# Second layer's experts: the odd batches' additions move from VectorE to GpSimd

## The reference, cut to what matters

```python
def _L1_ffn_ref(hidden_states, gate_w, w1, b1, w2, b2):
    x = hidden_states.reshape(-1, h)
    gate_probs = jax.nn.softmax(x @ gate_w.T, axis=-1)
    expert_idx = jnp.argmax(gate_probs, axis=-1)
    expert_w = jnp.take_along_axis(gate_probs, expert_idx[:, None], axis=1)[:, 0]
    for e in range(n_experts):
        ye = jax.nn.relu(x @ w1[e] + b1[e]) @ w2[e] + b2[e]
        sel = (expert_idx == e)[:, None]
        out = out + jnp.where(sel, ye * expert_w[:, None], 0.0)
...
x = x + jnp.tanh(g_ffn[1]) * _L1_ffn_ref(_layernorm(x, axis=-1), L1_ffn_gate_w, ...)
x = x + jnp.tanh(g_xattn[2]) * _L2_xattn_ref(_layernorm(x, axis=-1), ctx_1024, ...)
```

## Time and profile before

| | us |
|---|---|
| median of 3 runs | 1598.94 |
| lowest and highest of them | 1594.63, 1601.74 |
| the profiled execution | 1602.53 |
| its span (first to last instruction) | 1600.8 |
| PE, DVE, ACT, POOL busy | 1386.6, 953.2, 664.8, 422.6 |

### The profile page before, as it was taken

How to read it: one execution, slowest core, us unless ns; L and a number is a source line. 1 busy time by engine, 2 the same in 40 slices (tenths; PEclk the granted TensorE clock), 3 DMA queues, 4 the chain that set the end, 5 groups by cost and what they waited for, 6 DMA issues and landing times. The chain is left out here.

```text
span 1600.8 us, 31601 instructions
## 1 busy us (share of the span) xinstructions
PE 1386.6 (87%) x10662; PEld 1150.0 (72%) x10662; DVE 953.2 (60%) x2331; ACT 664.8 (42%) x1313; POOL 422.6 (26%) x578
## 2 busy tenths in 40 slices
PE   8999878889999994999999998999999997401588
PEld 5888645677799983788888887779999996400245
DVE  4888665666422225777777774832222265688887
ACT  3666453420344430333333334335555522430277
POOL 1000000012122210122221221246666633421141
PEclk9999999899799997999999998889999999755799
DMA  3000020673111107111111202012333344421001
GB/s 107 21 20 15 6 92 1 218 268 61 60 34 41 34 22 226 62 51 49 49 47 32 44 1 93 1 52 92 92 93 93 86 173 134 108 19 10 1 14 40
DMA packets 105328, 106.53 MB, mean 67 GB/s; under 512 B 36080, under 2 KB 92160, under 8 KB 105088
## 3 DMA queue, kind: packets, MB, share of 16 engines
q1 hardware_dynamic: 89312, 70.91, 14.6%
q0 software_dynamic: 11136, 28.93, 6.6%
q10 hardware_dynamic: 4768, 5.25, 1.1%
HBM read 83.19 MB, written 20.71 MB: 65 GB/s over the span
## 5 line engine op out<-in xcount | busy, mean ns | idle before, releaser
L3598 PEld LDWEIGHTS L2f_bank<-L2f_xT,L2f_w_tile 128*128 128x128 f32 x1264 | 154.5, 193 | 7.4 <-ACT L2f_xT L3662 3.4
L3598 PE MATMUL L2f_bank<-L2f_xT,L2f_w_tile 128*128 128x128 f32 x1264 | 155.2, 276 | 3.0 <-ACT L2f_xT L3662 3.0
L785 POOL TENSOR_TENSOR L2x_probs<-L2x_probs,L2x_inv_sum 128x512 f32<-128x512 f32 x64 | 66.3, 1057 | 268.4 <-DVE L2x_inv_sum L1062 268.4
L3712 DVE TENSOR_TENSOR L2f_hT<-L2f_gate_h,L2f_bank 128x256 f32<-128x256 f32 x79 | 33.3, 421 | 148.5 <-ACT L2f_gate_h L3669 148.5
L3521 POOL DMA_INDIRECT L2f_y_rows<-L2f_xn,L2f_put_row x79 | 78.2, 989 | 55.2 <-DVE L2f_xn L3728 51.6
L3656 ACT COPY L2f_w_tile<-L2f_w_up 128x1024 f32 x79 | 82.7, 1046 | 17.4 <-issue 17.4
L3513 POOL DMA_INDIRECT L2f_rows<-L2f_x_rows,L2f_take_row x79 | 77.0, 975 | 44.7 <-DVE L2f_take_row L3496 21.3
L3598 PEld LDWEIGHTS L1f_bank<-L1f_xT,L1f_w_tile 128*128 128x128 f32 x736 | 85.6, 192 | 1.1
L3598 PE MATMUL L1f_bank<-L1f_xT,L1f_w_tile 128*128 128x128 f32 x736 | 85.9, 275 | 0.0
L3615 PE MATMUL L1f_bank<-L1f_w_down,L1f_hT 128*128 x368 | 83.1, 379 | 0.0
L3615 PE MATMUL L2f_bank<-L2f_w_down,L2f_hT 128*128 x316 | 81.4, 380 | 0.1
(11 more groups left out here) (677 smaller groups left out, 3321.2 us busy)
## 6 DMA issues: line engine op xcount, KB each, us to landing
L1f_w_up<-in_L_ffn_w SPq DMA_DIRECT2D x16, 512.0 KB, 8.2
L1f_w_down<-in_L_ffn_w SPq DMA_DIRECT2D x16, 512.0 KB, 9.0
L2f_got<-L2f_y_rows SPq DMA_DIRECT2D x16, 512.0 KB, 4.4
L2f_w_up<-in_L_ffn_gate_w SPq DMA_DIRECT2D x16, 256.0 KB, 2.9
L2f_w_up<-in_L_ffn_up_w SPq DMA_DIRECT2D x16, 256.0 KB, 3.0
L2f_w_down<-in_L_ffn_down_w SPq DMA_DIRECT2D x16, 256.0 KB, 3.6
x<-in_x SPq DMA_DIRECT2D x4, 512.0 KB, 7.9
L0x_ctx<-in_ctx SPq DMA_DIRECT2D x16, 128.0 KB, 2.1
```

Of the source, the lines that this page charges most:

```text
L785: nc.gpsimd.tensor_tensor(probs[c][:, :, :], probs[c][:, :, :], inv_sum[:, c, :][:, :, None].to_broadcast([P, 4, P]), ALU.mult).then_inc(s ...
L3598: x = nc.tensor.matmul(products(j, m), w_tile[j][:, at:at + P], xT[j][:, k * P:(k + 1) * P], start=(k == 0), stop=(k == KT - 1))
L3712: nc.vector.tensor_tensor(hT[j][:, 0:F], gate_h[j][:, 0:F], bank[2 + j][:, F:2 * F], ALU.mult).then_inc(q["h"], 1)
```

## The change

The second layer's stage gets its own code. VectorE adds the even batches only, GpSimd the odd ones, in two instructions for a batch: a `tensor_scalar` that multiplies `got` by the share in place, and, after a wait for it, a `tensor_tensor` that adds it to `x`. VectorE keeps all 16 statistics; those of an odd batch wait for GpSimd's count `added_pool`. SyncE's loads of the pair r + 2 wait for the even addition of pair r on VectorE and for its odd addition on GpSimd. The third layer keeps its code.

```diff
-        g = core.sems_in(f"{tag}g", [f"got{j}" for j in range(4)] + ["added"])
+        g = core.sems_in(f"{tag}g", [f"got{j}" for j in range(4)] + ["added", "added_pool", "scaled_pool"])
...
-                after(sp, g["added"], 2 * K * (b // 2 - 1))
+                after(sp, g["added"], 2 * K * (b // 2 - 1) if gated else b // 2 - 1)
+                if not gated:
+                    after(sp, g["added_pool"], b // 2 - 1)
                 sp.dma_start(got[b % 4][:, :], ...
+
+        if not gated:
+            @block.gpsimd
+            def _(pool):
+                for b in range(1, B, 2):
+                    pool.wait_ge(g[f"got{b % 4}"], b // 4 * 16 + 16)
+                    nc.gpsimd.tensor_scalar(got[b % 4][:, 0:D], got[b % 4][:, 0:D], cols(pick_share, b, 1), None, ALU.mult
+                                            ).then_inc(g["scaled_pool"], 1)
+
+                    pool.wait_ge(g["scaled_pool"], b // 2 + 1)
+                    nc.gpsimd.tensor_tensor(cols(core.x, b * D, D), cols(core.x, b * D, D), got[b % 4][:, 0:D], ALU.add
+                                            ).then_inc(g["added_pool"], 1)
+
+            @block.vector
+            def _(dve):
+                for b in range(0, B, 2):
+                    dve.wait_ge(g[f"got{b % 4}"], b // 4 * 16 + 16)
+                    nc.vector.scalar_tensor_tensor(cols(core.x, b * D, D), got[b % 4][:, 0:D], cols(pick_share, b, 1),
+                                                   cols(core.x, b * D, D), ALU.mult, ALU.add).then_inc(g["added"], 1)
+                    if b >= 2:
+                        dve.wait_ge(g["added_pool"], b // 2)
+                        take_stats(core, b - 1)
+
+                    dve.wait_ge(g["added"], b // 2 + 1)
+                    take_stats(core, b)
+                dve.wait_ge(g["added_pool"], B // 2)
+                take_stats(core, B - 1)
+
+            phases.close()
+            return
```

## The result

| | before | after |
|---|---|---|
| median of 13 runs, us | 1600.69 | 1608.65 |
| lowest to highest | 1591.84 to 1609.78 | 1604.82 to 1615.46 |
| span of the profiled execution | 1600.8 | 1609.6 |

The ratio after to before is 1.0052 with a 95% interval of 1.0032 to 1.0071: the change costs 8 us, between 5 and 11. The forecast was 1602.4 us with a range to 1608.5, so the time lies 0.15 us outside. The miss is larger than that: the kernel before has a median of 1600.69 in these rounds, 1.75 above the 1598.94 that the forecast started from, so 8.0 us came where 3.5 were forecast.

A forecast was written before the change was run, and what follows sets the result against it. It took the buffer reload's round trip through GpSimd to bound the changed stage: +2.9 us, plus 0.6 for SBUF collisions, gives +3.5 on the median of 1598.94, so 1602.4 us, range 1595.5 to 1608.5.

The forecast's parts named there:

- The stage stands alone on the path: Second layer's stage: other engines wait at the barrier, so each microsecond it changes moves the whole rest of the program.
- The reload's round trip: Loads waiting for GpSimd's addition: 2.64 us to the new data plus 1.27 for GpSimd's batch, 3.91 us for two pairs.
- GpSimd idles between its pairs: Changed stage: GpSimd was to have 1 us or more of idle time in each round.
- Collisions: VectorE's additions and GpSimd's instructions meeting on SBUF, 0.19 to 0.40 us each, two on the path: 0.6 us.
- The other signs: Expected profile: first landing to last statistics 15 to 16.5 us, GpSimd's multiplications 3.9 us apart, TensorE's barrier wait 22 us.
- I take 0.49, since the new one has less to do than either: GpSimd's multiplication by a column, priced at 0.49 us from rows of nearest form, with 0.81 as upper end.
- The upper bound: GpSimd's batch at up to 2.08 us and landings of 2.6 us, making the effect at most +8.1 us.
- The part on edits that cost nothing: End of the stage: last statistics to next stage stays 1.11 us; two more semaphores cost below 0.05 us.
- the third: Measurably slower: GpSimd's two instructions and VectorE's addition exclude each other on SBUF at every pair; +8.1 us, 1607.0; chance 0.12.

The follow-up runs named there:

- kernels with 16 buffers: 16 buffers for the second layer's result rows, so no load waits: kernel before, interval 13.03 us; changed kernel with early drain and two-operation multiplication, 13.34 us.
- kernel with both repairs: Changed kernel with GpSimd drained early, behind the last scatter, and 0.0 added as the multiplication's second operation: interval 17.11 us; whole program 1603.06 us.
- kernel with five batches: Changed kernel with 16 buffers, early drain and two-operation multiplication, GpSimd taking five batches and VectorE eleven: interval 12.94 us; whole program 1599.79 us.

## Why the prediction was wrong

**What held.** The stage stands alone on the path: its 9.2 us came out as 8.8 in the span. The reload's round trip is the bound of the changed stage. From GpSimd's addition to the new odd data I had 2.64 us, and 2.62 to 2.72 were measured. GpSimd idles between its pairs (1.00, 0.76, 0.74 us), if less than the forecast's 1 us or more. The addition takes 0.72. With the two terms below taken out, the stage is 3.7 us longer than before, where the forecast had 3.5. The kernels with 16 buffers show that this remainder is indeed the reload: with it gone, so are the 3.7, the order of the statistics aside.

That 3.7 lies so near to 3.5 is in part luck. In the kernel with both repairs the way through the stage began later than I had it: GpSimd's first multiplication started 0.63 us after VectorE's first addition (604.65 - 604.02), where I had let batch 1's data be there after 0.42. The three reloads took 8.17 us and not 7.92. Collisions took 0.4 and not 0.6, and the last statistics 0.05 less, which pays most of that back.

The other signs came out beside the forecast as the time did: the stage up to the last statistics took 18.2 us and not 15 to 16.5, the rounds 4.4 and not 3.9, and TensorE waited 28.0 us and not 22.

**What was mis-sized: the multiplication.** The step reads "I take 0.49, since the new one has less to do than either". Both rows that I took for nearest, 0.486 and 0.55, are two-operation forms. The single-operation form was slower here and not faster: 0.924, against 0.478 for the same multiplication with a second operation. The trace of before had a row of that form, with an immediate in place of the column. I didn't look for it, since it stood under another name in the last layer:

```profile
L2651 POOL TENSOR_SCALAR ruler<-ruler x1: 876/876/876, 1377.6 to 1377.6; 128x256 f32<-128x256 f32 x1
```

With it the batch on GpSimd costs 1.73 us and not 1.27 (608.62 to 610.35), and enters five times. The runs put this at 2.1 us. The upper bound had room for it, the value didn't.

**What was left out: the drain.** The part on edits that cost nothing priced the way from the last statistics to the next stage at its 1.11 us, "barrier and clearing together". That was its price with GpSimd long since in the barrier. The change brings GpSimd's last operation to 0.46 us ahead of VectorE's, and its drain, which ends 3.9 us behind that operation, had been covered before, by the wait for the first load and by VectorE's 12 us. It costs 3.36 us (4.46 - 1.10), as three kernels show: one where nothing but a memset is added, one where nothing but a drain ahead of GpSimd's work is added, and the one with both repairs. The rule that the prediction itself followed for other edits, to name the work that hides a cost and ask what it costs when that cover is gone, wasn't applied to the barrier. Its row stood in the trace of before, 5025 ns on GpSimd's queue.

**Collisions.** They were priced at 0.6 us. In the changed kernel one multiplication was stretched from 0.92 to 1.09, two others by 0.04 and 0.02, and no addition of GpSimd's was, so on the path it was some 0.2. Three of VectorE's additions (at 608.04, 612.35 and 616.84) fell where GpSimd idled and took 0.48, and three (at 609.84, 614.43 and 618.73) started while GpSimd added and were stretched themselves, to 0.80, 0.56 and 0.60, off the path. Where both engines are busy throughout (16 buffers), GpSimd's instructions are stretched by some 0.9 us. In the changed kernel the three stretched additions of VectorE ended at 610.64, 614.99 and 619.33, 0.29, 0.28 and 0.28 us behind the end of GpSimd's addition. In the two places shown of the kernel with five batches VectorE's addition, having started 0.21 and 0.15 us behind GpSimd's start, ended 0.28 us behind its end as well, as the one of 1.49 us in the third layer's stage did.

**The sum again, as measured:** 3.7 (reload, with collisions, in the kernel with both repairs) + 2.1 (multiplication) + 3.4 (drain) = 9.2 us. The forecast had the first alone. Of the rivals, the third, slower than 2 to 6 us, named collisions as its mechanism, and that wasn't it.

## What to carry to other kernels

Before work is given to an engine that has been idle at the end of a stage, look at what that engine does between its last instruction and the barrier: here its drain ended 3.9 us behind its last instruction, at 603.5 before and at 624.8 after. In this program a GpSimd that had issued indirect DMAs owed 3.9 us (second layer) and 4.4 us (third layer) at its next drain. So look for that row, and drain GpSimd while it waits anyway, or leave it out of the stage's end. And take the price of an instruction from a row of the same form, down to the number of its operations, since here the form with less to do was the slower one (924 ns against 478).

## What the runs showed of the hardware that I had not expected

- GpSimd's drain in a stage with its own DMAs ended 3.84 to 3.86 us behind its last operation in the second layer's stage, whether that was a scatter, an addition or a memset of 98 ns, and even 21 us after the last DMA. An explicit drain took 5023 ns, over the last scatter and behind it, and the next one ended 0.1 us beyond the last operation. In the third layer's stage the kernel before has a like one: GpSimd's drain, 5097 ns from 1342.9, ends at 1348.0, 4.4 us behind its last addition and 0.75 us behind VectorE's last statistics (1347.24). From there to the next stage's first instruction (1349.05) go 1.81 us, where the second layer's stage has 1.10, so there some 0.7 us of it are already exposed. An early drain there wasn't tried. What sets the 3.9 us (the number of DMAs, or the queue's state) stays open.
- GpSimd's `tensor_scalar` of 128x256 floats with one operation took 924 ns (876 with an immediate, once), and with a second one that adds 0.0 it took 478 ns.
